# A mixed attention and feed-forward kernel on one core: its slot map in bf16 parts, its last transposes later, its last output tile apart

## Chip, cores, metric

One core of one Trainium2 chip runs the whole program in one launch. The metric is the time of one execution on the device in microseconds (us), the median of several runs. Arrays come from and go to the chip's memory (HBM) in float32.

## What is computed

1024 tokens (4 batches of 256) of width 256 go through four residual stages. Stage 2, a mixture of experts, is the long one.

```python
x = x + xattn0(layernorm(x), ctx, ...)         # softmax of normalised similarities
x = x + moe(layernorm(x), ...)                 # below
x = x + xattn1(ctx, ctx, mask, pad, layernorm(x), ...)
x = x + ghost_ffn(layernorm(x), lut, ...)      # h = silu(gate) * up, then down; 688 wide

# moe: E = 8 experts, K = 2 per token, cap = 160 slots for each expert and round k
top_p, top_i = lax.top_k(softmax(xt @ gate_w), K)
for k in range(K):
    e = top_i[:, k]; w = top_p[:, k]
    pos = cumsum(one_hot(e))[own column] - 1   # place of the token in its expert's queue
    keep = pos < cap
    h = gelu(buf @ w1 + b1)                    # buf: the kept tokens, by expert and place
    y = h @ w2 + b2 + gelu(buf @ wd) @ wu      # wd, wu: rank 32
    out += y[e, pos] * keep * w
out += 0.2 * (gelu(xt @ sw1 + sb1) @ sw2 + sb2 + gelu(xt @ swd) @ swu)   # shared expert
```

## The kernel before

The code is written by hand for each engine: every engine has its own list of instructions, in the order of the source, and they meet at semaphores (`wait_ge`, `then_inc`). There is no scheduler. A wait on an engine holds up all that is behind it on that engine.

Stage 1 (to about 33 us) is the first attention. Stage 2 runs in ten *units*: unit 0 is the shared expert on the first 512 tokens, units 1 to 8 are the eight experts on 320 slots each (two rounds of 160), unit 9 is the shared expert on the other 512 tokens. A unit has nine steps (STEPS = 9). In step s TensorE (PE) runs `first` (six matmuls into a PSUM bank `hb`, line 780: weights split in a high and a low part, `w_hi`, `w_lo`, and tokens too), ScalarE (ACT) applies Gelu (line 1095), and two steps later TensorE runs `second` of that step (line 799, plain float32, into the banks `yb`). VectorE (DVE) makes `w_lo` for the weights six steps ahead (`weights_lo`, line 1580), the low part of the transposed tokens (`rows_lo`, line 1351) and the low part of the rank-32 rows (`low_rows`, line 1587), without which `second` of step 0 can't start. In the units 1 to 8 VectorE also decodes the weights of stage 4 from a table (`lookup`, lines 1212 to 1280).

During unit 0 the kernel also finds out which token goes to which slot. For each half of the tokens (512 of them, 4 tiles of 128, two rounds: HT2 = 8 columns) the steps are: `choose` (top two experts on VectorE), `count` on TensorE (line 725 on: bf16 matmuls that number the tokens of an expert), `route` and `map_rows` on VectorE, and `slot_map` on TensorE (line 739). `map_rows` builds for each column a 128x128 one-hot of the slot's low seven bits (`lane_oh`, line 1449) and a row of 48 values (`map_in`, line 1460): for 8 experts and 3 chunks of 128 slots, the token's row number and its gate weight. `slot_map` multiplies the two in float32 and adds up over the columns; what comes out says for each slot which row it holds and with which weight. `map_half` and `map_done` read it; `row_of` (line 1479) is the list of rows by which GpSimd (POOL) gathers the tokens of an expert from HBM (line 538, three DMAs of 128, 128 and 64 rows). Two more small matmuls (`third_rows`, line 748) bring the third chunk into another layout. `expert_rows(1)` transposes the gathered tokens of unit 1 (line 692) and stands on TensorE between the last two `second` of unit 0.

Stage 4 is the last layer, with 24 *groups* n: four batches b of six groups f. For each n TensorE runs `gate_up` (line 925: 12 matmuls, 6 in the last, narrow group of a batch), ACT the Silu, VectorE the product as high part and whole (lines 1666, 1667), GpSimd the low part (line 573), and TensorE three groups later `down` (line 940: six matmuls). A batch begins with `transpose_x3` (line 904), ACT's copy (line 962), VectorE's low part (`x3T_split`, line 1644). The normalised tokens of a batch come late: stage 3's softmax (`attend`, exps on ACT, `add_probs`, `norm_x`) of batches 2 and 3 is woven into stage 4 between the groups, and ACT has to load its tables anew for it. `finish` (line 1651) adds a batch's result to x; the sync engine (SP) sends it out (line 432).

## Time and profile before

| | us |
|---|---|
| median of 3 runs | 305.8 (305.75 to 312.18) |
| the profiled execution | 306.0 |
| its span, first to last instruction | 304.2 |
| TensorE busy | 290.8 |
| VectorE busy | 240.4 |
| ScalarE busy | 155.3 |
| GpSimd busy | 116.5 |

The span is what the trace covers; 1.8 us of the execution's time lie around it. Busy time of TensorE is that of its matmuls, the weight loads run beside them. Starts in the trace are counted from the beginning of the span.

### The profile page before, as it was taken

Reading aid. Unit: us, or ns where it says so; the run is one execution under the profiler, and the core shown is the slowest. Engines: PE = TensorE matmul, PEld = TensorE weight load, DVE = VectorE, ACT = ScalarE, POOL = GpSimd, SP = SyncE. Lnnn points to the kernel's source line nnn. Section 1 sums busy time; section 2 is a strip of 40 time slices with the busy share of each in tenths; the row PEclk is TensorE's granted clock in tenths of the full one; section 3 lists DMA queues with packets and bytes.
Section 4 is the critical chain, followed back from the end, with each engine's and each line's share of the span. In section 5 each row is a group of like instructions: output and inputs, shape, how many; then the busy total and the mean of one; then the engine's idle time right before and its main releaser. Section 6 shows DMA issues by size and latency. Waiting matters only on the chain.

```text
span 304.2 us, 5858 instructions
## 1 busy us (share of the span) xinstructions
PE 290.8 (96%) x1911; PEld 253.1 (83%) x1911; DVE 240.4 (79%) x638; ACT 155.3 (51%) x369; POOL 116.5 (38%) x143
## 2 busy tenths in 40 slices
PE   7988998998999999999999999999999999989895
PEld 5545686977888998989989898999888899979795
DVE  4888878638989888889888898898985768796632
ACT  2677986225554755546556465555533633535210
POOL 7427410150518165280743806042061224443431
PEclk9999999999999999999999999999999999999999
DMA  7933207540958539195482935647044000010101
GB/s 214 328 139 95 80 0 230 171 138 5 296 163 221 172 79 349 52 253 174 101 286 61 291 134 131 209 78 226 1 43 140 0 1 2 0 37 0 37 0 69
DMA packets 21841, 38.06 MB, mean 125 GB/s; under 512 B 3131, under 2 KB 12411, under 8 KB 21820
## 3 DMA queue, kind: packets, MB, share of 16 engines
q1 hardware_dynamic: 17340, 32.55, 32.5%
q0 software_dynamic: 4480, 5.25, 9.2%
q8 instruction: 11, 0.18, 0.2%
q14 instruction: 10, 0.08, 0.1%
HBM read 31.37 MB, written 6.42 MB: 124 GB/s over the span
## 4 chain that ended last, share of the span: by engine, by line
PE 74%; DVE 12%; ACT 7%; issue 2%; POOL 2%; DMA 1%; SPq 0%; DVEq 0%; ACTq 0%
PE yb L799 27%; PE hb L780 27%; PE yb L814 6%; PE hb L925 4%; PE tb L692 4%; PE yb L940 1%; POOL rstd L454 1%; PE rb L940 1%; DVE xn L1195 1%; PE yb L925 1%; DMA projw<-projw_dram 1%; ACT sm L982 1%; DVE bst L1189 1%; DVE h L1667 1%; DVE x L1338 1%
## 5 line engine op out<-in xcount | busy, mean ns | idle before, releaser
L799 PE MATMUL yb<-raw,h 128*128 128x256 f32 x384 | 96.3, 380 | 0.1
L1095 ACT ACTIVATE h<-hb,b 128x320 f32<-128x320 f32 (+1 forms) x80 | 44.5, 558 | 63.7 <-PE hb L780 59.0
L799 PEld LDWEIGHTS yb<-raw,h 128*128 128x128 f32 x384 | 69.0, 189 | 7.4 <-ACT h L1095 0.5
L780 PE MATMUL hb<-xT_hi,w_hi 128*128 128x320 f32 (+1 forms) x180 | 71.4, 397 | 0.5 <-ACT small L1099 0.5
L780 PE MATMUL hb<-xT_lo,w_hi 128*128 128x320 f32 (+1 forms) x180 | 58.7, 326 | 0.0
L780 PE MATMUL hb<-xT_hi,w_lo 128*128 128x320 f32 (+1 forms) x180 | 58.6, 325 | 0.0
L554 POOL DMA_INDIRECT xacc_dram<-ysb,row_of x16 | 28.5, 1778 | 77.8 <-ACT ysb L962 75.4
L1221 DVE COPY_PREDICATED pick<-bits,pick 128x544 int32<-128x544 uint8 x56 | 43.3, 774 | 0.6
L538 POOL DMA_INDIRECT xg<-xnorm_dram,row_of x24 | 28.7, 1197 | 34.4 <-DVE row_of L1479 17.8
L1580 DVE TENSOR_TENSOR w_lo<-raw,w_hi 128x256 fp32r<-128x256 f32 x84 | 34.7, 415 | 7.4 <-ACT w_hi L962 7.3
L780 PEld LDWEIGHTS hb<-xT_hi,w_hi 128*128 128x128 f32 x180 | 33.9, 188 | 5.1 <-issue 2.2
L962 ACT ACTIVATE w_hi<-raw 128x256 fp32r<-128x256 f32 x90 | 36.5, 407 | 0.1
L780 PEld LDWEIGHTS hb<-xT_hi,w_lo 128*128 128x128 f32 x180 | 34.0, 189 | 2.4
L780 PEld LDWEIGHTS hb<-xT_lo,w_hi 128*128 128x128 f32 x180 | 33.8, 188 | 1.5
L1217 DVE TENSOR_SCALAR pick<-bit,lut_x,lut 128x544 int32<-128x544 int32 x64 | 34.8, 564 | 0.0
L573 POOL TENSOR_TENSOR h_lo<-h,h_hi 128x256 fp32r<-128x256 f32 x24 | 17.7, 742 | 30.3 <-DVE h L1667 30.3
L1351 DVE TENSOR_TENSOR xT_lo<-tb,xT_hi 128x320 fp32r<-128x320 f32 (+1 forms) x22 | 11.0, 541 | 14.6 <-ACT xT_hi L962 11.3
L925 PE MATMUL hb<-xT_hi,gw_hi 128*128 128x256 f32 x68 | 19.8, 291 | 1.2 <-DVE xT_lo L1644 1.1
L925 PE MATMUL hb<-xT_hi,gw_lo 128*128 128x256 f32 x68 | 19.1, 281 | 0.0
L925 PE MATMUL hb<-xT_lo,gw_hi 128*128 128x256 f32 x68 | 19.1, 280 | 0.0
L1189 DVE BATCH_NORM_STATS2 bst<-x 128x6 f32<-128x256 f32 x32 | 13.3, 416 | 6.1 <-DMA x<-xacc_dram 3.0
L962 ACT ACTIVATE xT_hi<-tb 128x320 fp32r<-128x320 f32 (+1 forms) x26 | 11.7, 496 | 10.8 <-PE tb L904 6.4
(226 smaller groups left out, 512.5 us busy)
## 6 DMA issues: line engine op xcount, KB each, us to landing
raw<-w1pack_dram SPq DMA_DIRECT2D x30, 384.0 KB, 4.9
raw<-w2pack_dram SPq DMA_DIRECT2D x30, 384.0 KB
idx<-idx_dram SPq DMA_DIRECT2D x8, 272.0 KB
x<-x_dram SPq DMA_DIRECT2D x4, 256.0 KB, 4.7
xnorm_dram<-xn SPq DMA_DIRECT2D x2, 512.0 KB, 5.8
xacc_dram<-x SPq DMA_DIRECT2D x2, 512.0 KB, 8.4
x<-xacc_dram SPq DMA_DIRECT2D x4, 256.0 KB, 3.9
out_dram<-x SPq DMA_DIRECT2D x4, 256.0 KB, 2.1
```

Of the source, the lines that this page charges most:

```text
L538: gp.indirect_dma_start(xg[0:n, turn, c, :], None, t["xnorm"], bass.IndirectOffsetOnAxis(ap=row_of[0:n, u - 1, c:c + 1], axis=0))\
L554: gp.indirect_dma_start(t["xacc"], bass.IndirectOffsetOnAxis(ap=row_of[:, u - 1, c:c + 1], axis=0), ysb[:, c, :], None, compute_op=ALU.add ...
L573: gp.tensor_tensor(h_lo[:, r, 0:S], product(r), h_hi[:, r, 0:S].bitcast(F32), ALU.subtract)\
L780: mm = pe.matmul(hb[s % RING][:, 0:n], w[:, s, k * P:(k + 1) * P], a[:, turn, k, 0:n], start=(i == 0), stop=(i == len(terms) - 1))
L799: mm = pe.matmul(yb[c // 2][:, (c % 2) * D:(c % 2 + 1) * D], h, w, start=(s == 0 and c % 2 == 0), stop=(s == STEPS - 1), skip_group_check= ...
L814: mm = pe.matmul(yb[1][half * H:(half + 1) * H, 0:P], hidden(s - 1, False, turn)[:, rows] if s > 0 else low_third[:, turn, :], raw2[:, tur ...
L925: mm = pe.matmul(ffn_banks[n % GRING][:, part * S:(part + 1) * S], w[:, at:at + P], a[:, b % 2, k, 0:S], start=(i == 0), stop=(i == len(te ...
L962: return act.activation(dst, src, ACT.Copy, scale=scale)
L1095: act.activation(hidden(s - 1, shared, turn), bank[:, 0:n], ACT.Gelu, bias=b1[:, expert, s - 1:s])\
L1217: dve.tensor_scalar(dst, bit0[:, :], lut_x[:, n:n + 1], lut_i[:, 2 * n:2 * n + 1], ALU.bitwise_and, ALU.bitwise_xor).then_inc(lk, 1)
L1221: dve.copy_predicated(dst, m, src).then_inc(lk, 1)
L1580: dve.tensor_tensor(w_lo[:, slot, :], raw1[:, slot, :], w_hi[:, slot, :].bitcast(F32), ALU.subtract)\
```

## The change

Slot map. The float32 matmuls of the slot map become bf16 matmuls. A row number is split in two parts that bf16 holds exactly (token in its tile minus slot's low bits; tile minus 128 times chunk), a gate weight in three parts. `lane_oh`, `map_in` and the constants are bf16. Rows and weights are now separate: `slot_rows(half)` has 16 matmuls of 24 columns for each half, added up over both halves in one bank; `slot_weights` has 16 matmuls of 72 columns for both halves together, later. In VectorE's list `map_rows` no longer waits for the gate's exponentials and no longer computes weights; the new `weight_rows` does that for both halves at once (seven short dependent instructions, three of 48 and three of 384 elements), after the row list is out. `third_rows` becomes `third_slots`, called for rows and for weights apart. In `choose` the two subtractions for the exponentials stand behind the one-hot.

Order in unit 0. `count(1)` stands after half of `second(4)`; `slot_rows(1)` after `second(5)`. In unit 1 VectorE's `low_rows` stands ahead of the table decoding.

Last layer. The transposes of batches 2 and 3 stand behind the last `gate_up` of the batch before, followed by two `down` in a row. `finish` of a batch stands one group later on VectorE, behind `x3T_split`. The second output tile of the last batch accumulates in a bank of its own (`tb[0]`); each of the two last tiles is added and sent out by itself.

```diff
-            def slot_map(half):
-                pe.wait_ge(map_in_ok, half + 1)
+            def slot_rows(half):
+                pe.wait_ge(row_in_ok, half + 1)
                 for n in range(HT2):
-                    mm = pe.matmul(maps[half], lane_oh[half][:, n, :], map_in[half][:, n, :, :]...,
-                                   start=(n == 0), stop=(n == HT2 - 1))
-                mm.then_inc(map_mm, 1)
...
+                    for v in range(2):
+                        mm = pe.matmul(row_map, lane_oh[half][:, n, :], row_parts[half][:, v, n, :], ...)
+                mm.then_inc(row_mm, 1)
+            def slot_weights():
+                pe.wait_ge(weight_in_ok, 1)
+                pe.wait_ge(third_row_ok, 1)
+                for n in range(T * TOPK):
+                    mm = pe.matmul(weight_map, lane_oh[n // HT2][:, n % HT2, :], weight_parts[:, n, :, :]..., ...)
+                mm.then_inc(weight_mm, 1)
...
                         elif s == 6:
+                            second(u, s - LAG, shared, turn, loads, range(0, 2))
                             count(1)
-                        elif s == 7:
-                            slot_map(1)
-                        elif s == 8:
-                            third_rows()
...
                         elif s == 6:
-                            slot_map(0)
+                            slot_rows(0)
+                        elif s == 7:
+                            slot_rows(1)
+                        elif s == 8:
+                            third_slots(0)
...
             second(0, STEPS - 2, True, 0)
+            slot_weights()
             expert_rows(1, 1)
             second(0, STEPS - 1, True, 0)
+            third_slots(1)
...
+                        apart = b == B - 1 and i == 1
+                        out = tb[0][:, 0:D] if apart else down_banks[b % 2][:, i * D:(i + 1) * D]
...
-                if n >= GLAG:
+                if n == 2 * NG - 1 or n == 3 * NG - 1:
+                    transpose_x3(n // NG + 1)
                     down((n - GLAG) // NG, (n - GLAG) % NG)
-                if n % NG == 4 and n // NG + 1 < B:
-                    transpose_x3(n // NG + 1)
+                    down((n - GLAG + 1) // NG, (n - GLAG + 1) % NG)
+                elif n >= GLAG and n != 2 * NG and n != 3 * NG:
+                    down((n - GLAG) // NG, (n - GLAG) % NG)
+                if n == NG - 2:
+                    transpose_x3(1)
...
# VectorE
-                weights(half)
...
                 elif s == 3:
-                    map_half()
+                    rows_done()
+                    weight_rows()
                 elif s == 5:
-                    map_done()
-                elif s == 6:
-                    third_done()
+                    third_rows_done()
+                elif s == 8:
+                    weights_done()
...
-                    if s == 1 and u:
+                    if s == 1 and u and not after_shared:
                         low_rows(u, UTOK if shared else SLOTS)
...
+                    if s == 0 and after_shared:
+                        low_rows(u, SLOTS)
...
                 if f == 4 and b + 1 < B:
                     x3T_split(b + 1)
+                if f == 4 and b > 0:
+                    finish(b - 1)
...
-                if f == 3 and b > 0:
-                    finish(b - 1)
-            finish(B - 1)
+            last = 2 * B - 2
+            dve.wait_ge(last_tile_mm, 1)
+            dve.tensor_tensor(x[:, last, :], x[:, last, :], down_banks[(B - 1) % 2][:, 0:D], ALU.add)...
+            dve.wait_ge(down_mm, B * NG)
+            dve.tensor_tensor(x[:, last + 1, :], x[:, last + 1, :], tb[0][:, 0:D], ALU.add)...
```

How TensorE's list changes in unit 0, steps 6 to 8. First the list before, from the end of `count(1)`: L799 is `second`, L739 `slot_map`, L780 `first`, L748 `third_rows`; the file's `pick` and `h` hold `map_in` and `lane_oh`.

```order
L799 MATMUL yb<-raw,h 128x256 [waits h32_ok]
L799 MATMUL yb<-raw,h 128x256 x3
L739 MATMUL rb<-pick,h 128x48 [waits map_in_ok]
L739 MATMUL rb<-pick,h 128x48 x7
L780 MATMUL hb<-xT_hi,w_hi 128x512 [waits h32_ok,w_lo_ok]
...
L739 MATMUL tb<-pick,h 128x48 [waits map_in_ok]
L739 MATMUL tb<-pick,h 128x48 x7
L799 MATMUL yb<-raw,h 128x256 [waits h32_ok]
L799 MATMUL yb<-raw,h 128x256 x3
L780 MATMUL hb<-xT_hi,w_hi 128x512 [waits h32_ok,w_lo_ok]
...
L748 MATMUL tb<-pick,ident 64x16 [waits map_read]
```

The same place in the changed kernel: L830 is `second`, L744 the first matmul of `count(1)`, L759 `slot_rows`, L811 `first`.

```order
L830 MATMUL yb<-raw,h 128x256 [waits h32_ok]
L830 MATMUL yb<-raw,h 128x256
L744 MATMUL tb<-onehot,before 128x64 [waits onehot_ok]
...
L830 MATMUL yb<-raw,h 128x256 [waits h32_ok]
L830 MATMUL yb<-raw,h 128x256
L759 MATMUL rb<-pick,h 128x24 [waits row_in_ok]
L759 MATMUL rb<-pick,h 128x24 x15
L811 MATMUL hb<-xT_hi,w_hi 128x512 [waits h32_ok,w_lo_ok]
...
L830 MATMUL yb<-raw,h 128x256 [waits h32_ok]
L830 MATMUL yb<-raw,h 128x256 x3
L759 MATMUL rb<-pick,h 128x24 [waits row_in_ok]
```

`count(1)` now has half of `second(4)` ahead of it, and the second map has all of `second(5)` between `first(7)` and itself. TensorE further on, to unit 1: L778 is `third_slots`, L768 `slot_weights`, L711 `expert_rows(1)`.

```order
L830 MATMUL yb<-raw,h 128x256 [waits h32_ok,raw2_in0_2]
L830 MATMUL yb<-raw,h 128x256 x3
L778 MATMUL rb<-pick,ident 64x8 [waits sum_ok]
L778 MATMUL rb<-pick,ident 64x8
L830 MATMUL yb<-raw,h 128x256 [waits h32_ok]
L830 MATMUL yb<-raw,h 128x256 x3
L768 MATMUL rb<-pick,h 128x72 [waits third_row_ok,weight_in_ok]
L768 MATMUL rb<-pick,h 128x72 x15
L711 MATMUL tb<-ident,xg 128x128 [waits xg_in1,third_row_ok,xT_lo_ok]
...
L778 MATMUL rb<-pick,ident 64x8 [waits sum_ok]
L778 MATMUL rb<-pick,ident 64x8
L811 MATMUL hb<-xT_hi,w_hi 128x320 [waits h32_ok,w_lo_ok,xT_lo_ok]
```

`slot_weights` stands in front of the transposes of unit 1 and waits for two things of VectorE.

VectorE at the start of unit 1, before: L1521 the gate weights of the unit, L1580 `w_lo`, L1228 to L1217 the decoding, L1587 `low_rows`.

```order
L1580 TENSOR_TENSOR w_lo<-raw,w_hi 128x256 [waits w_hi_ok]
L1228 TENSOR_SCALAR bit<-idx 128x544 [waits idx_in]
L1214 TENSOR_SCALAR bits<-idx 128x544 x3
L1587 TENSOR_TENSOR lowrank<-small,lowrank 32x320 [waits low32_ok,low_hi_ok,lk]
L1580 TENSOR_TENSOR w_lo<-raw,w_hi 128x256 [waits w_hi_ok]
L1217 TENSOR_SCALAR pick<-bit,lut_x,lut 128x544 x2
```

And now: L1587 the gate weights, L1648 `w_lo`, L1655 `low_rows`, L1270 to L1259 the decoding.

```order
L1587 COPY wsel<-wmap 128x3 [waits wmap_ok]
L1648 TENSOR_TENSOR w_lo<-raw,w_hi 128x256 [waits w_hi_ok]
L1655 TENSOR_TENSOR lowrank<-small,lowrank 32x320 [waits low32_ok,low_hi_ok]
L1270 TENSOR_SCALAR bit<-idx 128x544 [waits idx_in]
L1256 TENSOR_SCALAR bits<-idx 128x544 x3
L1648 TENSOR_TENSOR w_lo<-raw,w_hi 128x256 [waits w_hi_ok,lk]
L1259 TENSOR_SCALAR pick<-bit,lut_x,lut 128x544 x2
```

`low_rows` has moved ahead of four decoding instructions.

TensorE at the end of batch 1 in the last layer, before: L904 the transposes of batch 2, L925 `gate_up` (of groups 11, 12, 13), L940 `down` (8, 9).

```order
L904 MATMUL tb<-ident,xn 128x128 [waits x3T_lo,x3n_ok]
L904 MATMUL tb<-ident,xn 128x128 x3
L925 MATMUL yb<-xT_hi,gw_hi 128x256 [waits prod_ok]
...
L940 MATMUL yb<-gw_hi,h_hi 128x256 [waits g_lo_ok]
...
L925 MATMUL hb<-xT_hi,gw_hi 128x256 [waits x3T_lo,prod_ok]
...
L940 MATMUL yb<-gw_hi,h_hi 128x256 [waits g_lo_ok]
...
L925 MATMUL hb<-xT_hi,gw_hi 128x256 [waits prod_ok]
```

And now: L959 is `gate_up` (11, 12, 13), L938 the transposes, L976 `down` (8, 9).

```order
L959 MATMUL yb<-xT_hi,gw_hi 128x256 [waits prod_ok]
...
L938 MATMUL tb<-ident,xn 128x128 [waits x3T_lo,x3n_ok]
L938 MATMUL tb<-ident,xn 128x128 x3
L976 MATMUL yb<-gw_hi,h_hi 128x256 [waits g_lo_ok]
...
L976 MATMUL yb<-gw_hi,h_hi 128x256 [waits g_lo_ok]
...
L959 MATMUL hb<-xT_hi,gw_hi 128x256 [waits x3T_lo,prod_ok]
...
L959 MATMUL hb<-xT_hi,gw_hi 128x256 [waits prod_ok]
```

The transposes have moved behind `gate_up(11)`, and `down(9)` ahead of `gate_up(12)`. The same happens a batch later, with groups 17 to 19 and `down` 14 and 15.

## Rows read from the trace of the kernel before

**Rows 1.** The page, busy time of each engine (share, instructions) and the clock granted to TensorE.

```profile
PE 290.8 (96%) x1911; PEld 253.1 (83%) x1911; DVE 240.4 (79%) x638; ACT 155.3 (51%) x369; POOL 116.5 (38%) x143
PEclk9999999999999999999999999999999999999999
```

**Rows 2.** Waits of TensorE: engine, line, releaser; total us, times, longest.

```profile
PE tb L904 <- DVE xn L1195: 1.8, 2, 0.9
PE yb L799 <- DVE lowrank L1587: 1.4, 1, 1.4
PE hb L925 <- DVE xT_lo L1644: 1.1, 2, 0.5
PE tb L725 <- DVE onehot L1400: 1.0, 1, 1.0
```

**Rows 3.** Chain that ended last, 48 to 92 us: start us, us, what.

```profile
51.66 0.17 PE tb L731 x7
...
53.66 1.72 PE rb L739 x16
55.38 1.45 PE hb L780 x6
...
58.55 1.80 PE yb L799 x8
...
68.53 0.89 PE hb L780 x6
```

**Rows 4.** Timeline, unit 0, 51 to 62 us: start us, us, engine, line, instruction.

```profile
51.69 1.97 PE L799 MATMUL yb<-raw,h 128*128 128x256 f32 x8
...
54.66 0.18 DVE L1426 TENSOR_REDUCE lrs<-lexp 128x4 f32<-128x32 f32 x1
...
55.29 0.28 DVE L1454 TENSOR_TENSOR pick<-pick,vw 128x24 f32<-128x24 f32 x2
...
55.60 0.63 DVE L1460 TENSOR_TENSOR pick<-onehot,pick 128x192 f32<-128x192 bf16 x2
...
58.59 0.18 DVE L1479 TENSOR_TENSOR row_of<-pick,tb 128x24 uint32<-128x24 f32 x1 [1.18 <-PE tb L739]
...
59.08 1.25 POOL L538 DMA_INDIRECT xg<-xnorm_dram,row_of  x1 [17.84 <-DVE row_of L1479]
```

**Rows 5.** Windows: stretch us, busy us of PE, PEld, DVE, ACT, POOL, clock, DMA share, GB/s.

```profile
63.50:64.00 0.50, 0.50 (x4) 0.44 (x3) 0.24 (x1) 0.00 (x0) 0.50 (x1) 1.00 0.41 131
```

**Rows 6.** Timeline, start of unit 1, 70 to 74 us.

```profile
70.91 0.43 DVE L1580 TENSOR_TENSOR w_lo<-raw,w_hi 128x256 fp32r<-128x256 f32 x1 [0.97 <-ACT w_hi L962]
...
71.74 0.31 PE L780 MATMUL hb<-xT_lo,w_hi 128*128 128x320 f32 x1
...
72.77 0.48 DVE L1587 TENSOR_TENSOR lowrank<-small,lowrank 32x320 fp32r<-32x320 f32 x1
...
73.40 0.48 PE L799 MATMUL yb<-w_up,lowrank 128*128 128x256 f32 x2 [1.35 <-DVE lowrank L1587]
```

**Rows 7.** Timeline, last layer, 268 to 286 us.

```profile
268.48 0.66 PE L904 MATMUL tb<-ident,xn 128*128 128x128 f32 x4 [0.83 <-DVE xn L1195]
...
269.17 0.60 ACT L962 ACTIVATE xT_hi<-tb 128x512 fp32r<-128x512 f32 x1 [1.80 <-PE tb L904]
...
276.67 0.42 DVE L1666 TENSOR_TENSOR h_hi<-h,hb 128x256 fp32r<-128x256 f32 x1 [2.35 <-ACT h L1174]
...
283.26 0.66 PE L904 MATMUL tb<-ident,xn 128*128 128x128 f32 x4 [0.93 <-DVE xn L1195]
...
285.88 0.36 PE L925 MATMUL hb<-xT_hi,gw_hi 128*128 128x256 f32 x1 [0.54 <-DVE xT_lo L1644]
```

**Rows 8.** Timeline, last addition, 300 us.

```profile
300.92 0.69 DVE L1651 TENSOR_TENSOR x<-x,yb 128x512 f32<-128x512 f32 x1 [1.89 <-PE yb L940]
```

**Rows 9.** The page, DMA issues: queue, operation, count, KB each, median us from issue to landing.

```profile
raw<-w1pack_dram SPq DMA_DIRECT2D x30, 384.0 KB, 4.9
...
out_dram<-x SPq DMA_DIRECT2D x4, 256.0 KB, 2.1
```

More of the change, by code:

```diff
@@ L429, in _ @@
                              t["xacc"][S * b:S * b + S, :].rearrange("(i p) d -> p i d", p=P)).then_inc(x_back[b], 16)
-            for b in range(B):
+            for b in range(B - 1):
                 sp.wait_ge(x4_ok, b + 1)
@@ L433, in _ @@
                     .then_inc(out_done, 16)
-            sp.wait_ge(out_done, 16 * B)
+            for i in range(2):
+                sp.wait_ge(x4_ok, B + i)
+                sp.dma_start(t["out"][B - 1, i * P:(i + 1) * P, :], x[:, 2 * B - 2 + i, :]).then_inc(out_done, 16)
+            sp.wait_ge(out_done, 16 * B + 16)
         @block.gpsimd
```

185 lines of the change are left out of this document (116 added, 69 removed).

## Prediction

> **What bounds the kernel now.** I read the page first. TensorE is busy 290.8 of 304.2 us and its clock is at the upper of its two levels, 2.4 GHz, in every slice; VectorE has 240.4 us [rows 1]. So only two things can shorten the run: fewer microseconds of TensorE work, or fewer of the 13.4 us in which it has none. The waits of TensorE say where those are: 1.8 us for the normalised tokens of the last layer, 1.4 us for `low_rows` in unit 1, 1.1 us for the low part of the last layer's transposed tokens, 1.0 us for the one-hot of `count(1)` [rows 2]. The change is aimed at all four places. The chain of waits then gives the prices on TensorE: 1.72 us for one `slot_map` (the reader is to see 16 records for eight matmuls: a float32 matmul goes through the array in two parts, and there are two maps), 1.45 for a `first`, 1.80 for a `second`, and unit 1 starting at 68.2 [rows 3]. The timelines give what VectorE and GpSimd do beside it.
>
> **Part 1: unit 0, about -2.7 us.** (a) The 1.0 us wait at `count(1)` [rows 2]. The matmul began at 51.45, so TensorE had come there at 50.45. Half a `second(4)`, 0.9, now goes first, so it asks at 51.35; the one-hot is done earlier than before, since `map_rows(0)` has lost three dependent steps on VectorE (about 0.6, from 54.66 to the products at 55.29 in its twin for half 1 [rows 4]) and gained two short ones (0.2), and two subtractions now stand behind it (0.2). Gain 0.95. (b) The maps: before 2 x 1.72 = 3.44. Now 16 + 16 + 16 = 48 bf16 matmuls with their own weight loads. The nearest rows are the bf16 matmuls of `count`: seven take 0.17, 24 ns each [rows 3], and from the first of the eight at 51.45 to the `second` at 51.69 [rows 4] it is 30 ns each. They are 16 to 64 columns wide, the new ones 24 or 72. I take 30: 1.44. The ends are 24 ns (1.15) and the pace of the float32 parts, 1.72/16 = 108 ns (5.2). Gain 2.0, from -1.7 (a loss) to 2.3. (c) `third_slots` twice instead of once: 0.22 more, the length in which the one before ends. Sum 0.95 + 2.0 - 0.22 = 2.7.
>
> The Trainium skill, page TensorE: Matmul & The Clock Gate, section LDWEIGHTS, gives a load as columns / 1.2 ns, 107 ns for 128 columns; section Weight-path perf modes says that bf16 loads of full width measured about twice as fast. By the first the 48 would take 5.1 us, by the second 2.6, against my 1.44. The rows of `count` speak against both, at 30 ns.
>
> What has to hold so that nothing waits anew. *Row parts of half 1:* before ready at 55.60 + 0.63 = 56.2 [rows 4]; now 0.1 earlier from `count`, 0.6 for the weights not computed, 0.1 for a subtraction gone, 0.2 added: 55.6. TensorE comes at 51.35 + 0.35 + 0.9 + 0.5 + 1.4 + 1.7 = 56.2. It holds by 0.6. *Third row and weight parts:* the second map ends at 56.7 instead of 58.55, VectorE writes the row list, then `weight_rows`: seven dependent steps at 0.21 (three took 0.63, from 54.66 to 55.29 [rows 4]) = 1.5; three products of 48 elements, 0.45; three of 384, twice the elements of the 0.63 for two [rows 4], so 0.5 each, 1.5. If bf16 is no faster than float32 that is 3.45, if the long ones halve, 2.7; I take 3.4 and reach 60.4. Two `w_lo` and the third row bring 61.3. TensorE comes to `slot_weights` at 56.7 + 1.4 + 1.75 + 0.2 + 1.7 = 61.8. It holds by 0.5; behind this wait stand the transposes and all of unit 1. *Gathered tokens:* the row list was out at 58.77 and the last third of the gather landed before 64.0 (131 GB/s in that half microsecond is 65 KB, its 64 rows of 1 KB [rows 5]), so 5.2 later. Now it is out at 56.9, the landing at 62.1; TensorE asks at 61.8 + 0.5 = 62.3. This is the thinnest cover, 0.2, and each microsecond it lacks costs one.
>
> **Part 2: unit 1, -1.35 us.** TensorE ended `first(3)` at about 71.9 (last matmul begun 71.74) and waited to 73.40; `low_rows` ran at 72.77 because four decoding instructions stood ahead, from 71.25 [rows 6]. Now it follows `w_lo` of 70.91, starts at 71.3 and ends at 71.8, when TensorE comes. Gain 1.35 of the 1.4 in the waits, 1.1 to 1.5. Is it given back? VectorE has some 16.4 us of work in unit 1, and TensorE now takes 15.1 for the unit instead of 16.45. But VectorE starts its share later and hands over ahead: its parts for unit 2 had some 2 us to spare there, now 0.7 to 1, and in each later unit, with the third block on TensorE too, it catches up. So I count nothing.
>
> **Part 3: last layer, -0.9 us.** Waits at both transposes (0.83 and 0.93) and at both first groups of a batch (0.54 each) [rows 7]: 2.84 in all. They do not all go, since the tokens come from a loop over VectorE and ACT, which sets its own pace. At batch 2, TensorE does `gate_up(11)` (0.7) in the first wait, transposes at 268.5, does `down(8)`, waits 0.3 for the low part of group 9, does `down(9)` and starts `gate_up(12)` at 270.65 instead of 271.08, with `down(9)` behind it: 1.1 ahead. But `finish` now stands between `x3T_split` and `attend`, and ACT's copy (to 269.77 [rows 7]) holds `x3T_split`, so `attend` starts 0.2 later, the exponentials and ACT's two table loads end 0.2 later, and the product of group 12, at 276.67 before [rows 7], comes at 276.9. TensorE waits for it. The transposes of batch 3 come at 283.26 + 0.2 = 283.45; `gate_up(17)` is done by then, then `down(14)`, `down(15)`, and `gate_up(18)` starts at 285.65 instead of 285.88 [rows 7], with `down(15)` (0.7) behind it. 0.23 + 0.7 = 0.9. From here on to the end nothing waited. Ends: 0.2, if the exponentials slip further; 1.4, if they do not slip.
>
> **Part 4: the end, -0.45 us.** Now 0.69 us for 512 columns, begun at 300.92 [rows 8], then a DMA of 256 KB, 2.1 us [rows 9]. The first tile's addition begins three matmuls earlier and is over when the second one's begins; that takes 0.41, the price of 256 columns in the twin at 276.67 (0.42 [rows 7]): 0.27 saved. The second DMA has 128 KB: between nothing and the 0.37 us that half of the bytes took; its issue may wait some 0.1 behind the first's. I take 0.2. Ends 0.1 and 0.65.
>
> **Sum.** 2.7 + 1.35 + 0.9 + 0.45 = 5.4. The profiled execution took 306.0 with 304.2 of span; 306.0 - 5.4 = 300.6. The median of the runs shown is 305.8, so this is 1.7% under it. A measurement of this kernel can tell about 2% from no change, that is 299.7.
>
> **Rivals.** *A, the bf16 matmuls load slower than the rows of `count` say.* For it: there the weights are the same block each time but the first, here 48 different ones, and the moving rows are so short that nothing hides a load. Against it: the trace shows a load for each. At the float32 pace, 108 ns, 3.7 more: 304.3; at half of that 301.8. *B, the last layer gives nothing,* because the loop attend, exponentials, table loads, products is what bounds it from group 10 on, and a later `finish` delays it: for it speaks ACT's two table loads between the products, against it that `down(15)` is work that has to be done anyway and is now done in a wait. 300.6 + 0.9 = 301.5. *C, all covers hold and the ends are the good ones:* 2.95 + 1.5 + 1.3 + 0.65 = 6.4, 299.6. *D, slower.* `weight_rows` stands ahead of the `w_lo` that releases the w1 load of unit 2, so that load is issued 3.5 us later, at about 61. ACT needs it for the fourth `w_hi` in unit 1, at about 69.5, and behind that stand all Gelus of the unit. A load takes 4.9 [rows 9], up to 61 + 4.9 = 66. From a landing later than 8.5 us after issue it stalls ACT and with it TensorE; to end slower than before it has to be 5.4 later still, 14 us. Nothing in the trace is near it. The price: 306 or more. *E, the change doesn't do what it says:* `slot_weights` waits for VectorE or for the gather and gives back what (a) brought: 301.6.
>
> **Chances.** Forecast 0.58, A 0.10, B 0.11, C 0.10, D 0.03, E 0.08. The forecast's own spread is some 0.8 us to either side, so about a sixth of it also lies under 299.7, which with C gives 0.20 for faster by over 2%. Slower by over 2% would need D, 0.02; the rest, 0.78, lies within 2%. The range goes from 299.4, C's end, to 302.6, which takes in B, E and A's milder half.
>
> **What would show it.** Right: the 48 bf16 matmuls in three blocks of about 0.5 us; no wait at `count(1)`; the row list near 56.9; unit 1 from 65.4 on; no wait of TensorE for `low_rows`; units 2 to 8 as long as before; in the last layer a wait of about 1.4 at the second transposes, 0.3 to 0.5 at `down(9)` and `down(12)`; the last addition 0.4 long. Wrong: the blocks at 0.9 us or more; a wait of TensorE for the gather or for the third row; new waits for `w_lo` or for the tokens of unit 2, which would mean that VectorE had no room; the product of group 12 later than 277.2, counted in the old time.

## The result

The changed kernel takes 304.37 us (median of 12 runs, 301.61 to 311.23), the kernel before 305.85 (12 runs on the same chip). Some executions of either kernel take several microseconds more (two of the 12 before, four of the 12 after); the ratios, groups and ranges of times given from here on leave them out, the medians do not. The ratio is 0.9901, with a 95% interval of 0.9882 to 0.9919: 1% faster, within 2%. The forecast was 300.6 with a range of 299.4 to 302.6, so the median lies 1.8 us outside it. The sign was right, the size was not: of 5.4 us, 1.5 came by the medians and 3.0 (2.5 to 3.6) by the ratio. Before, the times lie within 0.3 us of each other but for one at 306.8; after, they fall into two groups, near 302.0 (five) and near 304.4 (three). The first group lies under the upper end of the range, and is still 1.4 over the forecast. The profile is of the second group: 304.5 us, of which 302.7 are span.

The page of the kernel after, busy time of each engine and the clock:

```profile
PE 290.1 (96%) x1931; PEld 251.9 (83%) x1931; DVE 243.2 (80%) x647; ACT 155.2 (51%) x369; POOL 116.3 (38%) x144
PEclk9999999999999999999999999999999999999999
```

TensorE is busy 0.7 us less than before [rows 1] and idle 12.6 us instead of 13.4. (From 48.4 us to the start of unit 1, where the maps stand, its busy time fell by 1.5, from 18.7 to 17.2; in the first 20 us, before any changed step of TensorE, it happened to be 0.7 more.) So the work went as wanted, the waits hardly. Where they are now, waits of TensorE:

```profile
PE tb L711 <- DMA xg<-xnorm_dram,row_of: 2.5, 1, 2.5
PE yb L830 <- ACT h L1137: 1.4, 1, 1.4
...
PE tb L938 <- DVE xn L1237: 1.1, 1, 1.1
```

All four waits of [rows 2] are gone or smaller: none for `lowrank`, none for `xT_lo` in the last layer, none for the one-hot, and 1.1 instead of 1.8 for the tokens. In their place stand one of 2.5 for the gather (unit 1's transposes) and one of 1.4 for ACT in unit 9. Together 3.9, as much as the whole distance between 300.6 and 304.5.

The chain that ended last, 52 to 72 us (start us, us, what), as [rows 3]:

```profile
52.43 0.39 PE rb L759 x16
52.82 1.50 PE hb L811 x6
...
56.04 0.40 PE rb L759 x16
...
56.47 0.19 DVE row_of L1535
56.66 0.80 issue
57.46 1.25 POOL xg L557
...
60.38 4.27 DMA xg<-xnorm_dram,row_of
...
64.78 1.19 PE tb L711 x6
...
68.11 3.74 PE hb L811 x24
```

Each of the two blocks of `slot_rows`, 16 bf16 matmuls, takes 0.39 to 0.40, 25 ns a matmul, where the float32 maps took 1.72 each. The step that writes the row list starts at 56.47 and ends at 56.65 (58.59 and 58.77 before [rows 4]; forecast for the end 56.9). And yet unit 1 begins at 68.11 (68.2 before): the third gathered tile, issued at 60.38, lands 4.27 later, eight after the list was out. Two views show what stands beside it. SyncE's queue: the w1 load of unit 2, in two thirds back to back, 60.9 to 62.4 (before, one was issued at 57.44 and the other at 63.25):

```profile
60.86 1.49 SPq L397 DMA_DIRECT2D raw<-w1pack_dram  x2
```

and the windows (stretch, busy us of PE, PEld, DVE, ACT, POOL, clock, DMA share, GB/s), to be read against [rows 5]:

```profile
63.00:63.50 0.50, 0.00 (x0) 0.00 (x0) 0.00 (x0) 0.00 (x0) 0.39 (x1) 1.00 0.97 383
63.50:64.00 0.50, 0.00 (x0) 0.00 (x0) 0.00 (x0) 0.00 (x0) 0.50 (x1) 1.00 0.85 277
```

Unit 1 is as forecast: the step for `low_rows` follows the first `w_lo`, and `second` no longer waits (73.40 with 1.35 of a wait before [rows 6]):

```profile
71.16 0.48 DVE L1655 TENSOR_TENSOR lowrank<-small,lowrank 32x320 fp32r<-32x320 f32 x1
...
71.79 0.48 PE L830 MATMUL yb<-w_up,lowrank 128*128 128x256 f32 x2
```

From here to unit 9 the kernel is 1.6 us ahead. There 1.3 of them go. The chain, unit 9:

```profile
226.52 4.07 DMA x<-xacc_dram
...
230.68 0.44 DVE bst L1231
...
239.42 1.28 ACT L1137
...
240.72 0.70 ACT h L1137
...
241.46 1.99 PE yb L830 x8
...
245.62 0.49 PE hb L959 x4
```

The tokens are read back 4.1 us after the issue (2.8 before), VectorE prepares the attention of batches 0 and 1, ACT does the exponentials and loads its table again (239.42), and only then comes the Gelu for which TensorE waits. The last layer starts its first gate group at 245.39, against 245.69.

In the last layer TensorE's last matmul begins at 299.26 against 300.61, so the layer gave 1.05. The tail, from that start to the end of the span, is 3.48 against 3.57. The additions in it:

```profile
299.22 0.42 DVE L1765 TENSOR_TENSOR x<-x,yb 128x256 f32<-128x256 f32 x1 [1.53 <-PE yb L976]
299.57 0.42 DVE L1767 TENSOR_TENSOR x<-x,tb 128x256 f32<-128x256 f32 x1
```

The first addition begins before the last matmul does, and the second 0.31 behind the start of that matmul, as the single one did before (300.92 against 300.61 [rows 8]), and it is 0.27 shorter. So VectorE's part came as forecast. What ends the program is something else. At the end of the whole program (the trace files it under line 65, the `with` that holds it) each engine has closing steps, and the last of them come only when all engines are through. First before, then after (engine, operation, count, its length in ns three times, and its start):

```profile
L65 POOLq DRAIN  x1: 4780/4780/4780, 299.1 to 299.1; - x1
L65 SPq COMPARE_BRANCH  x1: 37/37/37, 303.8 to 303.8; - x1
```

```profile
L65 POOLq DRAIN  x1: 4780/4780/4780, 297.7 to 297.7; - x1
L65 SPq COMPARE_BRANCH  x1: 38/38/38, 301.9 to 301.9; - x1
```

SyncE comes past its wait for the stores 3.17 after the start of the last matmul before and 2.62 after the change: 0.55 earlier. But GpSimd's DRAIN takes 4.78 us and ends 3.25 after that start in both. Before, the stores were over within 0.1 us of it; now they are over 0.6 before it, and the span ends 0.2 after it.

### The profile page after: what moved, and what is told of

Same layout as the page of the kernel before. It is cut to its first block, busy times and chain, and to the rows that moved or that the text cites. A ratio compares the mean times of both kernels' runs of the same rounds, so it can differ in the third digit from the quotient of the medians.

```text
span 302.7 us, 5910 instructions
## 1 busy us (share of the span) xinstructions
PE 290.1 (96%) x1931; PEld 251.9 (83%) x1931; DVE 243.2 (80%) x647; ACT 155.2 (51%) x369; POOL 116.3 (38%) x144
## 4 chain that ended last, share of the span: by engine, by line
PE 69%; DVE 11%; ACT 7%; DMA 5%; POOL 4%; issue 3%; SPq 0%; DVEq 0%; POOLq 0%; ACTq 0%
PE hb L811 25%; PE yb L830 24%; PE yb L845 5%; PE hb L959 4%; PE tb L711 4%; DVE bst L1231 1%; POOL rstd L472 1%; DMA xg<-xnorm_dram,row_of 1%; DMA x<-xacc_dram 1%; DVE xn L1237 1%; PE rb L976 1%; DMA xacc_dram<-ysb,third_row 1%; PE yb L959 1%; ACT sm L1024 1%; DMA projw<-projw_dram 1%
## 5 line engine op out<-in xcount | busy, mean ns | idle before, releaser
L830 PE MATMUL yb<-raw,h 128*128 128x256 f32 x384 | 96.5, 379 | 1.4 <-ACT h L1137 1.4
L830 PEld LDWEIGHTS yb<-raw,h 128*128 128x128 f32 x384 | 69.1, 189 | 8.8 <-ACT h L1137 1.8
L811 PE MATMUL hb<-xT_hi,w_hi 128*128 128x320 f32 (+1 forms) x180 | 71.2, 396 | 0.5 <-ACT small L1141 0.5
L811 PE MATMUL hb<-xT_lo,w_hi 128*128 128x320 f32 (+1 forms) x180 | 58.7, 326 | 0.0
L811 PE MATMUL hb<-xT_hi,w_lo 128*128 128x320 f32 (+1 forms) x180 | 58.6, 326 | 0.0
L1648 DVE TENSOR_TENSOR w_lo<-raw,w_hi 128x256 fp32r<-128x256 f32 x84 | 34.5, 415 | 6.6 <-ACT w_hi L1004 6.5
L811 PEld LDWEIGHTS hb<-xT_hi,w_hi 128*128 128x128 f32 x180 | 33.9, 189 | 5.1 <-issue 2.2
L1004 ACT ACTIVATE w_hi<-raw 128x256 fp32r<-128x256 f32 x90 | 36.5, 407 | 0.1
L811 PEld LDWEIGHTS hb<-xT_hi,w_lo 128*128 128x128 f32 x180 | 34.0, 189 | 2.4
L811 PEld LDWEIGHTS hb<-xT_lo,w_hi 128*128 128x128 f32 x180 | 33.8, 188 | 1.6
L1259 DVE TENSOR_SCALAR pick<-bit,lut_x,lut 128x544 int32<-128x544 int32 x64 | 35.0, 567 | 0.0
L959 PE MATMUL hb<-xT_hi,gw_hi 128*128 128x256 f32 x68 | 19.5, 287 | 0.1
L1004 ACT ACTIVATE xT_hi<-tb 128x320 fp32r<-128x320 f32 (+1 forms) x26 | 11.7, 496 | 14.9 <-PE tb L711 7.6
L959 PE MATMUL hb<-xT_hi,gw_lo 128*128 128x256 f32 x68 | 19.1, 281 | 0.0
L959 PE MATMUL hb<-xT_lo,gw_hi 128*128 128x256 f32 x68 | 19.1, 280 | 0.0
```

Source lines behind the costliest of these rows:

```text
L811: mm = pe.matmul(hb[s % RING][:, 0:n], w[:, s, k * P:(k + 1) * P], a[:, turn, k, 0:n], start=(i == 0), stop=(i == len(terms) - 1))
L830: mm = pe.matmul(yb[c // 2][:, (c % 2) * D:(c % 2 + 1) * D], h, w, start=(s == 0 and c % 2 == 0), stop=(s == STEPS - 1), skip_group_check= ...
L959: mm = pe.matmul(ffn_banks[n % GRING][:, part * S:(part + 1) * S], w[:, at:at + P], a[:, b % 2, k, 0:S], start=(i == 0), stop=(i == len(te ...
L1004: return act.activation(dst, src, ACT.Copy, scale=scale)
L1259: dve.tensor_scalar(dst, bit0[:, :], lut_x[:, n:n + 1], lut_i[:, 2 * n:2 * n + 1], ALU.bitwise_and, ALU.bitwise_xor).then_inc(lk, 1)
L1648: dve.tensor_tensor(w_lo[:, slot, :], raw1[:, slot, :], w_hi[:, slot, :].bitcast(F32), ALU.subtract)\
```

## The experiments

**Is the late gather the late w1 load's doing?** Four kernels on one chip. `again` is the changed kernel. `e1_order` moves one call:

```diff
                     rows_done()
-                    weight_rows()
                 elif s == 5:
+                    weight_rows()
                     third_rows_done()
```

> The changed kernel as it is, a second profile. Its undisturbed times so far lie in two groups, near 302.0 and near 304.4 us, and the profile at hand is one of the second group, with a wait of 2.5 us for the gather in unit 1 and one of 1.4 us for ACT in unit 9. Theory C (the collision of the w1 load of unit 2 with the gather makes the wait, each time): both waits are there in a run of either group, the times differ by something else. Rival D (the gather lands late only in some executions): a profile of the first group has a wait for the gather under 0.5 us. Median 302 to 304.4.

> Only weight_rows moves, from behind the row list to behind the w_lo steps that release the w1 load of unit 2, so that load is issued near 57.5 again instead of 60.9, as in the old kernel. Theory C (contention with that load): the third gathered tile lands by 62.5 to 63, TensorE's wait for the gather falls from 2.5 to under 0.7 us, unit 1 starts at 65.8 to 66.3, and the time falls by 1.0 to 2.0 against the changed kernel (part of it may be eaten by unit 9, which had a new wait of 1.4). Rival G (a gather of three tiles takes 7 to 8 us when it starts so early, whatever else is loaded): the wait stays at 2 or more, and slot_weights perhaps waits for VectorE a little (0.2) besides.

`e2_hold` adds a wait on SyncE:

```diff
                     sp.wait_ge(w_lo_ok, (u - 1) * STEPS + 3 * q + 3)
+                    if u_is(u, 2) and q == 0:
+                        sp.wait_ge(xg_in[1], 48)
```

> The changed kernel, but SyncE issues the w1 loads of unit 2 only once the three gathered tiles have landed. Theory C: landing at 62 to 62.7, wait of TensorE for the gather under 0.5 us, and the loads, which go out near 62.5, are not missed by ACT (needed near 69.5): 1.0 to 2.3 us faster than the changed kernel in its slower group. Rival G (the gather itself is slow when issued at 57.5): landing stays at 64 to 64.6 and the wait at 2 or more; the time as the changed kernel's.

`e3_keep` puts the write of the rows ahead of the w2 loads:

```diff
+                if u_is(u, 1):
+                    keep_rows(1)
                 if u_is(u, 2):
                     sp.wait_ge(mm2, STEPS)
...
-            keep_rows(1)
             keep_x(1)
```

> The changed kernel, but the rows of the second half are written back to memory ahead of the three w2 loads of unit 1 instead of behind them. In the changed kernel the first gather starts 0.8 us after the row list (0.3 before the change), and the theory is that it waits for this write to land. Theory W: the first gather starts 0.3 after the row list, near 56.8, and the wait for the third falls by 0.5 to 0.6 or less, since the collision with the w1 load stays. Rival (the 0.8 is GpSimd's own): still 0.8. Time within 0.6 us of the changed kernel's.

Medians and ratios: again 303.61, 0.9911 (0.9882 to 0.9940); e1_order 302.63, 0.9900 (0.9872 to 0.9929); e2_hold 303.61, 0.9923 (0.9905 to 0.9941); e3_keep 304.40, 0.9931 (0.9910 to 0.9953). In the trace of again the gather is in time (transposes at 63.27, no wait) and unit 1 still starts only at 67.85: neither theory C nor rival D as I had put them. ACT and VectorE were late instead, which is shown below on another run. e1_order starts unit 1 at 65.78, near the forecast, with a wait of 1.8 in unit 9. e2_hold has no profile that can be compared; its times, 302.9 to 303.9, are no better than again's. In e3_keep the write went out at 47.39 instead of 48.73, and the first gather starts 0.49 after the row list, as in again: there the write held nothing back. In the first profile it seems to have done so: written at 49.00 and landed at 56.6, as the row list came out, with the gather 0.99 after the list. The one other profile with a late first gather (g_quiet below, 1.17) has the write landed at 56.7; in all the others (0.5) it had landed by 56.0. So the write can add 0.5 to 0.7, when it goes out late (the w2 loads ahead of it took 2.42 us to issue there, 1.38 before).

Two more readings bear on theory C. In the first profile the w1 load goes out 0.48 behind the third gather (60.38, 60.86); in again, e3_keep and the later profiles with the load near 61 to 62 it goes out 1.3 behind, and TensorE waits 0.2 at most. And where a w1 load goes out 0.5 behind the first gather (e6_both, h2_shift and h3_tail below), that gather lands 3.8 to 4.0 after its issue, in h1_quiet, with no load there, 3.0; the third gather lands in all four after 2.4 to 2.6. So the 4.27 of the first profile is probably the load's doing, but only because the gather had started late as well. That is one profile, and no experiment repeated it.

**The parts alone.** `p1_map` is the changed kernel with the other three parts put back as before. `p2_low` and `p3_last` are the kernel before with one part of the change each:

```diff
-                    if s == 1 and u:
+                    if s == 1 and u and not after_shared:
                         low_rows(u, UTOK if shared else SLOTS)
...
+                    if s == 0 and after_shared:
+                        low_rows(u, SLOTS)
```

```diff
-                if n >= GLAG:
-                    down((n - GLAG) // NG, (n - GLAG) % NG)
-                if n % NG == 4 and n // NG + 1 < B:
-                    transpose_x3(n // NG + 1)
+                if n == 2 * NG - 1 or n == 3 * NG - 1:
+                    transpose_x3(n // NG + 1)
+                    down((n - GLAG) // NG, (n - GLAG) % NG)
...
```

> Only the slot map part of the change; the step of low_rows, the last layer and the last tile stay as before. Theory C (as found in the changed kernel): TensorE gets through the maps 2.5 to 3 us earlier, then either waits about 2.5 for the gather or its partners (ACT, VectorE) come late, so that unit 1 starts within 0.5 us of before (68.2); the 1.4 wait for low_rows is still there; in all 0 to 0.6 us faster than before: 305.3 to 306. Rival (the gain of the map arrives in the executions without a collision): up to 2.5 faster, and the times spread over two groups.

> The kernel before with low_rows of unit 1 moved ahead alone. Unit 1 gets 1.3 to 1.6 us shorter. Theory U (unit 9 has no slack: ACT cannot do its Gelu before the attention of the last layer, which waits for the tokens read back, and these land 4.1 to 4.7 us after their issue in the changed kernel against 2.8 before): TensorE then waits 1.0 to 1.6 for ACT in unit 9 and the time is only 0 to 0.5 us under before, 305.3 to 305.9. Rival N (the landing was late by chance and the chain moves with TensorE): no wait in unit 9, 304.3 to 304.6.

> The kernel before with the order of the last layer changed alone (transposes behind the last gate group, the additions of a finished batch one step later). Nothing before unit 9's end moves. Theory L (what the changed kernel's trace shows: three of the four waits gone, one of 1.1 left at the transposes of batch 3): 1.2 to 1.4 us faster than before, 304.4 to 304.7. My forecast had 0.9 (304.9). Rival: the 1.4 needed the earlier or later arrival that the other parts bring, then 0.7 or less.

p1_map: 305.09, from 303.56 to 305.47 but for one at 307.05, ratio 0.9966 (0.9940 to 0.9993). Its profile is of the fastest group and shows the map at its full price: the first matmul of unit 1 at 65.72, 2.46 ahead of before.

```profile
65.72 0.42 PE L808 MATMUL hb<-xT_hi,w_hi 128*128 128x320 f32 x1
```

The rival there was right: the gain arrives in some executions. p2_low: 304.87, ratio 0.9965 (0.9942 to 0.9988); its last layer begins at 244.34 instead of 245.69, 1.35 ahead, and TensorE has no wait in unit 9. My theory U (no slack) falls: with a load that lands 2.8 after its issue, as in p2_low, the chain over the tokens read back moves with TensorE. What costs is a late landing. p3_last: 305.06, ratio 0.9974 (0.9961 to 0.9988); the layer alone (first gate group to last matmul) is 1.05 shorter, as in the changed kernel.

**Unit 9.** On top of e1_order, `e6_both` lets ACT do its last Gelus first, and VectorE what leads to the exponentials of batch 1 later:

```diff
                         exps(1, 0)
+                    if u_is(u, E + 1) and s == 8:
                         exps(1, 1)
...
                         combined(s - 5)
-                        attend(s - 5)
+                        if s == 5:
+                            attend(0)
...
                     add_probs(1, 0, 4)
+                    attend(1)
```

> The changed kernel with weight_rows behind the w_lo steps (as in e1_order) and two moves in unit 9: ACT does the exponentials of batch 1 behind its last Gelu instead of ahead of the last two, and VectorE prepares them behind the additions of batch 0. Theory U (TensorE's wait of 1.4 to 1.8 for ACT in unit 9 comes only from the exponentials of batch 1 standing ahead of the Gelu): no such wait, the transposes of batch 0 in the last layer with at most 0.4 of a wait, 1.3 to 1.8 us faster than e1_order: 300.6 to 301.2. Rival V (the normalised tokens of batch 0 are the real bound, through the tokens read back): the wait moves to the transposes and the gain is under 0.6.

It takes 300.98 (300.46 to 301.28), ratio 0.9834 (0.9810 to 0.9858). TensorE goes from `second` to the transposes without a wait:

```profile
236.74 2.75 PE L830 MATMUL yb<-raw,h 128*128 128x256 f32 x12
239.33 0.60 PE L938 MATMUL tb<-ident,xn 128*128 128x128 f32 x4
```

But its load had landed after 3.2 us, so this one run does not say what the moves are worth. The square of the two moves on one chip does (`e7_u9`: unit 9 alone on the changed kernel):

> The changed kernel once more, on one chip with the next three, as the corner of a square of two moves (weight_rows behind the w_lo steps; the two moves of unit 9). Theory M: two transfers land late by chance of the moment. The gathered tokens of unit 1, or the engines behind them, cost 2.3 us in some executions and nothing in others; the tokens read back in unit 9 cost 1.0 to 1.8 when a block of instructions (queue q8) passes inside the first of the four loads. So 304.4, 302.0 and, with neither, 300.6 are the places where its undisturbed times gather.

> As e1_order, weight_rows moved. Theory M: the 2.3 us in unit 1 never occur, unit 9 costs what its loads cost in f_after: its fastest times equal those of f_after, its slowest undisturbed ones lie 2 to 2.4 under the slowest of f_after; median 302.2. Rival (the position of weight_rows is not what decides, as e2_hold with its times of 302.9 to 303.9 may say): the same spread and median as f_after within 0.5.

> The changed kernel with the two moves of unit 9 alone (exponentials of batch 1 behind the last Gelu, their rows behind the additions of batch 0). Theory M: 1.0 to 1.6 us under f_after, both at its slow and at its fast end: 300.6 and 302.9 as the places of its times. Rival V (the wait moves on to the transposes of the last layer): under 0.6.

> Both moves, as e6_both. Theory M: one group of times at 300.4 to 301.0, 1.3 to 1.8 under f_e1, which is what the forecast promised for the changed kernel (300.6). No wait of TensorE over 0.5 us between 60 and 67 us, nor for ACT in unit 9.

Medians: f_after 304.38, f_e1 303.87, e7_u9 302.96, f_e6 302.80; ratios 0.9949 (0.9927 to 0.9970), 0.9929 (0.9903 to 0.9955), 0.9893 (0.9874 to 0.9912), 0.9890 (0.9871 to 0.9909). By the medians unit 9's moves bring 1.1 to 1.4 and the place of `weight_rows` at most 0.5 here; by the ratios 1.2 to 1.7 and at most 0.6. The traces say why. First load of unit 9, us from issue to landing, and TensorE's wait for ACT there: f_after 4.6 and 1.9, f_e1 3.1 and 0.2, f_e6 4.4 and none. The waits of TensorE in f_after:

```profile
PE yb L830 <- ACT h L1137: 1.9, 1, 1.9
...
PE hb L811 <- DVE xT_lo L1393: 1.0, 1, 1.0
```

and in f_e6, where the first of the two is not there and a small one has come in the last layer:

```profile
PE hb L811 <- DVE xT_lo L1394: 1.3, 1, 1.3
...
PE hb L959 <- DVE xT_lo L1717: 0.3, 1, 0.3
```

The other one is in unit 1, and it costs all three with a profile here 1.4 to 1.5 (first matmul at 67.2 to 67.3 against 65.8), f_e1 and f_e6 too, where `weight_rows` stands behind. Theory M, that this move takes the loss away, is refuted.

**What is late in unit 1.** Base and three variants of e6_both on one chip; `h1_quiet` is this edit, `h2_shift` adds 25 memsets on VectorE and 12 copies on ACT at the start, `h3_tail` has the old last tile:

```diff
                     sp.wait_ge(w_lo_ok, (u - 1) * STEPS + 3 * q + 3)
+                    if u_is(u, 2) and q == 0:
+                        sp.wait_ge(xT_hi_ok, 3 * DK)
...
+                if u == 2:
+                    gp.wait_ge(xT_hi_ok, 3 * DK)
                 if u > 2:
                     gp.wait_ge(xT_mm, u)
```

> e6_both once more, as the base of the next three on their chip: unit 1 starts at 65.8 (no loss) or at 67.2 (loss), 300.4 to 301.3 or 302.2 to 303.2.

> As the base, but the w1 loads and the gather for unit 2 start only when ACT has copied the transposed tokens of unit 1, so that the DMA engines are all but idle from about 62 to 64.5. Theory Q (transfers queued ahead cause the loss): unit 1 starts at 65.8 in the profile on whichever chip, and all undisturbed times lie in one group near 300.6 (or up to 1 more, if the w1 load now comes late for ACT near 69.5). Rival R (the loss is not from transfers): where the base shows unit 1 at 67.2, this one does too.

> As the base, with 25 short memsets on VectorE and 12 short copies on ACT in the first microseconds, where both engines wait for loads; they compute nothing that is used. Theory I (the loss is a late supply of instructions, at a fixed place of each engine's stream): the place moves by 12 to 25 instructions, and VectorE and ACT start their steps for unit 1 with no more than 0.1 us behind their semaphores; a late start may appear at another step. Rival: the late start stays at the same steps where the base has it. The added work itself: 0 to 0.3 us.

> As the base, with the last output tile as before the change (one addition of 512 columns, one store of 256 KB). My forecast: 0.45 slower than the base. Theory T (what the two traces show: from the start of the last matmul to the end of the span 3.57 us before and 3.48 after): 0.1 slower, within 0.2 of the base.

Medians 301.12, 300.92, 301.48, 301.46; ratios 0.9833 (0.9816 to 0.9850), 0.9836 (0.9822 to 0.9849), 0.9851 (0.9829 to 0.9872), 0.9851 (0.9829 to 0.9873). On this chip the base, by its times of 300.6 to 301.4, does not lose in unit 1, nor does any of the others (first matmul of unit 1 at 65.6 to 66.1), so h1_quiet and h2_shift told nothing of the cause: inconclusive. h3_tail's times can't tell 0.1 from 0.45, but its tail is 3.58 us from its last matmul, as before the change, against 3.48 in the changed kernel: theory T, 0.1. The DRAIN of GpSimd says why: 4.78 us here too, ended 3.26 after the start of the last matmul.

So the same transfers were taken from the changed kernel itself, with its base on the same chip:

> The changed kernel once more, as the base of g_quiet on the same chip: undisturbed times spread from about 302 to 304.6, most above 303.

> The changed kernel, but the w1 loads and the gather for unit 2 start only when ACT has copied the transposed tokens of unit 1 (weight_rows and unit 9 stay as in the changed kernel). Theory Q (those transfers, queued in front, cause the loss): unit 1 starts at 65.6 to 66.0, no wait of TensorE, ACT or VectorE over 0.5 us behind its last releaser from 62 to 66; all undisturbed times within 1.6 us (the rest is the wait in unit 9, 0.3 to 1.8), 301.0 to 302.4, median 1 to 2.5 under g_after. Rival R (it is not the transfers): the same spread and median as g_after within 0.5.

g_after 303.55, ratio 0.9918 (0.9896 to 0.9940); g_quiet 302.65, ratio 0.9889 (0.9874 to 0.9904). The times are 302.24 to 304.11 against 301.57 to 302.73, with 0.9 between the medians. The timeline of VectorE in g_after, start of unit 1:

```profile
62.62 0.50 DVE L1579 SCALAR_TENSOR_TENSOR w_up<-w_up,up_sign,raw 64x256 fp32r<-64x256 f32 x1
66.04 0.23 DVE L1542 TENSOR_REDUCE pick<-rb 128x24 f32<-128x72 f32 x1 [2.92 <-remote]
```

and its waits from 60 to 68 us:

```profile
ACT xT_hi L1004 <- remote: 6.8, 1, 6.8
DVE pick L1542 <- remote: 2.9, 1, 2.9
...
PE hb L811 <- DVE xT_lo L1393: 1.0, 1, 1.0
```

L1542 waits for one thing in the program, the end of `slot_weights`, which was there at 62.7; it starts 3.3 later, after 2.92 of idle time. ACT's copy (L1004) waits for the transposes, over at 64.0; it starts at 66.12. The releaser that the profile infers is none of the program's semaphores: "remote". In g_quiet, VectorE:

```profile
62.45 0.23 DVE L1546 TENSOR_REDUCE pick<-rb 128x24 f32<-128x72 f32 x1
```

and of TensorE and ACT, 60 to 68 us:

```profile
ACT xT_hi L1008 <- PE tb L715: 5.7, 1, 5.7
...
PE tb L715 <- DMA xg<-xnorm_dram,row_of: 1.1, 1, 1.1
```

The late start of both engines is gone, ACT is released by its transposes again, and unit 1 begins at 66.6 instead of 67.6. What is left is a wait of 1.1 for the gather, with nothing of unit 2 beside it: its write went out at 48.67, its first gather 1.17 after the row list. So theory Q does not hold for the gather. For VectorE and ACT the two profiles fit it, but do not prove it: they are one each, e6_both had no late start without any hold, the intervals of the two ratios overlap, and 0.5 of the 1.5 us between the two spans is unit 9's.

The kernel before and all kernels with the new map that have a profile to compare, in one table (us; "row list" is the start of the step that writes it; "late" is the idle time of VectorE ahead of its first step for unit 1 after all that the step waits for in the program was there; "landing" is of the first load in unit 9, from its issue):

| run | chip | row list | transposes, unit 1 | late | unit 1 from | landing | TensorE waits for ACT, unit 9 |
|---|---|---|---|---|---|---|---|
| before | a | 58.59 | 65.45 | - | 68.18 | 2.8 | - |
| after | a | 56.47 | 64.78, waited 2.5 | - | 68.04 | 4.1 | 1.4 |
| again | b | 57.23 | 63.27 | 1.4 | 67.85 | 4.5 | 1.7 |
| e3_keep | b | 57.31 | 63.22 | 1.4 | 67.91 | 4.7 | 1.9 |
| e1_order | b | 56.50 | 62.53 | 0.9 | 65.78 | 4.5 | 1.8 |
| p1_map | c | 56.52 | 62.46 | - | 65.72 | 3.2 | 0.3 |
| e6_both | c | 56.53 | 62.49 | - | 65.75 | 3.2 | - |
| f_after | d | 56.42 | 62.33 | 2.9 | 67.18 | 4.6 | 1.9 |
| f_e1 | d | 56.56 | 62.57 | 1.7 | 67.26 | 3.1 | 0.2 |
| f_e6 | d | 56.57 | 62.62 | 1.7 | 67.25 | 4.4 | - |
| h1_quiet | e | 56.44 | 62.34 | - | 65.59 | 4.2 | - |
| h2_shift | e | 56.65 | 62.65 | - | 65.91 | 4.5 | - |
| h3_tail | e | 56.74 | 62.80 | - | 66.06 | 4.6 | - |
| g_after | f | 56.84 | 62.84 | 2.9 | 67.60 | 3.2 | 0.4 |
| g_quiet | f | 56.40 | 63.35, waited 1.1 | - | 66.61 | 2.8 | - |

**The version that beats both** is e6_both, 301.0 to 301.1 on two chips (ratios 0.9834 and 0.9833) and 302.80 on the one where unit 1 started late (0.9890). With the hold of h1_quiet it is 300.92 (0.9836), no different, its five times within 0.7 us; whether the hold helps it where unit 1 starts late was not tried.

## Why the prediction was wrong, point by point

**Part 1 (a), (b), (c): right up to the maps' end, and 2.46 of 2.7 where nothing was late.** The bf16 matmuls took 25 ns each in the two row blocks and 32 in `slot_weights` (0.52 for the 16; forecast 30), no wait at `count(1)`, the row list out at 56.65 (forecast 56.9), `slot_weights` at 61.6 (forecast 61.8). Rival A is dead: p1_map, e1_order, e6_both, h1_quiet, h2_shift and h3_tail start unit 1 at 65.6 to 66.1, forecast 65.4.

**Part 1, the covers: the step that failed.** "Now it is out at 56.9, the landing at 62.1 ... This is the thinnest cover, 0.2." The cover was about as thin as that when things go well (TensorE starts its transposes at 62.3 to 62.8, on chip b up to 63.3, with 0.2 of a wait at most), though the 5.2 us from the list to the landing were read too short: in p2_low, which is the kernel before up to there, the third gather is issued at 62.05 and lands 2.5 later, 5.6 after the list was out. But I took this landing, from one trace, as if it were fixed. In the first profile it was at 64.65, 8.0 after the list. The write of the rows I had not priced at all, and the load for unit 2, which rival D had seen to move by 3.5 us, for its own consumer alone, not for what it may do to transfers in flight. And one cover I had not named: before, VectorE and ACT have their next step for unit 1 only at 66.6 to 67.2, 3.4 to 3.9 us after their last of unit 0; now they are wanted at 62.5 and 63.7, and of the eleven profiles with the new map, without a hold, in which TensorE itself was not kept by the gather, six show them 1.4 to 2.9 late (and e1_order VectorE 0.9, at no cost). The forecast's own list of what would prove it wrong had the wait for the gather, not this.

**Part 2: right**, 1.35 forecast, 1.35 in p2_low, about 1.5 in the changed kernel. "Is it given back? ... So I count nothing" holds for VectorE's room, and failed for a place that I had not looked at: unit 9, where before the Gelu ended just as TensorE came. In the traces with a landing of 2.7 to 3.2 after the issue the wait there is 0 to 0.4, in those with 4.1 to 4.7 it is 1.4 to 1.9, unless the order of unit 9 is changed; then it is 0 with landings of 4.2 to 4.6, and 0.3 comes back in the last layer.

**Part 3: right**, 0.9 forecast, 1.05 in the changed kernel and alone. One wait of 1.1 is left (forecast 1.4); rival B is refuted.

**Part 4: its own steps right, the tail 0.09 shorter instead of 0.45.** The last addition ended 0.26 earlier behind the last matmul (forecast 0.27), and with the stores SyncE was 0.55 earlier (forecast 0.45). What failed is a term that I had put at nothing: the closing steps of the other engines. GpSimd's DRAIN of 4.78 us ends 3.25 to 3.26 after the start of the last matmul in every profile compared here, and the span can't end before it. Before, it ended within 0.1 us of the stores and so did not show.

**Sum.** In the profiled run: unit 0 0.14 instead of 2.7, unit 1 1.5, unit 9 -1.3, last layer 1.05, tail 0.09: 1.44 of span. Without the two losses 2.46 + 1.35 + 1.05 + 0.09 = 4.95, that is 301.05, and e6_both, h0_base and h1_quiet, which avoid one and on their chips did not meet the other, take 300.9 to 301.1. That a sum fits to 0.1 is partly luck: these medians move by some tenths. Rival E had the right shape (given back at `slot_weights` or the gather, 301.6), too small a price, and no partner in unit 9.

**What stays open.** Why VectorE and ACT start late is not settled. The times suggest that the transfers for unit 2 matter (g_quiet against g_after), and the traces that it depends on the chip or the moment (f_e6 and e6_both are the same kernel: 67.25 and 65.75). One idea was a late supply of instructions: a queue of kind "instruction" (q8) moves blocks of some 16 KB through the same DMA engines, eleven in a run. The Trainium skill, page Advanced Engine Details and Errata, section ISA Cache, gives an engine other than TensorE 32 KB for its instructions, in only two lines of 16 KB, 256 instructions each. The block's size agrees (11 packets, 0.18 MB). If an engine that reaches a new line had to wait for a block that queues behind the loads, a late start and a block would belong together. The traces speak against it: in f_after, where VectorE is 2.9 late, no packet of kind "instruction" moves between 56 and 70 us, and in e3_keep, 1.4 late, none between 56.5 and 68. h2_shift, meant to move the place, ran where nothing was late.

Why the first load of unit 9 lands after 2.7 or after 4.7 us, with the same three loads issued behind it at the same distances each time, is open as well. In all nine profiles with 4.1 to 4.7 a packet of q8 starts 1.2 to 2.6 us after the issue of the load. Of the eight with 2.7 to 3.2 six have it at 2.7 or later, but g_quiet has it at 2.3 and f_e1 at 2.6, and their loads were not late. So the two go together more often than not, and no experiment moved the one without the other.

## What to carry to other kernels

A gain on the bounding engine arrives only as far as its partners' next steps can come forward: for each place where TensorE will ask earlier, write down what answers there (the gather, VectorE's and ACT's first step of the next unit, an exponential that stands ahead of a Gelu) and since when it could have answered. A cover of 0.2 us behind an indirect DMA is no cover; give a landing the spread it has over several profiles, and look at what releases the DMA's own start (here also a write). Where a step is put ahead of another on VectorE, follow the semaphores of the later one to the loads they release, and ask what those loads will fly beside, not only who needs them. Put what must not wait (the Gelu of the bounding chain) ahead of what hangs on a load. And before you shorten a tail, look which engine's closing step ends last, also among engines that have long been idle.

## What the runs showed of the hardware that I had not expected

A bf16 load of 128x128 weights with a matmul of 24 columns took 25 ns, with one of 72 columns 32 ns, 16 different weights one after another. bf16 did nothing for VectorE where operands are broadcast: the 128x1024 comparison took 1.22 us in both types. GpSimd's DRAIN at the end of the program took 4.78 us in every profile compared here, and began when its last product did. The same load of 256 KB, with the same three behind it, landed after 2.7 to 4.7 us. The same kernel showed a late start of VectorE and ACT by 1.7 us on one chip and none on another, with the loads issued at the same 57.5.
